# Projections in even half steps, later loads, gelu inputs in score banks, a new order at the end, and exponentials tile by tile

## The chip, the core and the metric

The kernel runs on one core of one Trainium2 chip. Its engines work side by side, each through a queue of its own in program order, and wait for one another by semaphores: TensorE (PE in the profile; its weight loads are PEld), VectorE (DVE), ScalarE (ACT), GpSimd (POOL) and SyncE (SP), which here only issues transfers. The metric is the device time of one launch in microseconds (us).

## What is computed

Two layers, each a gated cross attention of 16 heads and a gated feed-forward, on 4 batches of 512 tokens of width 256. The first feed-forward is a mixture of 8 experts of which each token takes two; the second rounds activations to 8 bits and weights to three values. Cut to what matters:

```python
x = x + tanh(g_xattn[0]) * xattn(layernorm(x), ctx, ctx, Wq, bq, Wk, bk, Wv, bv, Wo, bo)   # layer 0
x = x + tanh(g_ffn[0]) * moe(layernorm(x), router_w, router_b, expert_weights)
x = x + tanh(g_xattn[1]) * xattn(layernorm(x), ctx, ctx, ...)                             # layer 1
x = x + tanh(g_ffn[1]) * ffn(layernorm(x), w1, w2)

def xattn(query, key, value, ...):
    q, k, v = heads(query @ Wq.T + bq), heads(key @ Wk.T + bk), heads(value @ Wv.T + bv)  # 16 heads of 16
    weights = softmax(einsum('bhqd,bhkd->bhqk', q, k) / sqrt(16))
    return einsum('bhqk,bhkd->bhqd', weights, v) @ Wo.T + bo

def ffn(x, w1, w2):
    h = gelu(quant_act(x) @ quant_weight(w1).T)
    return quant_act(h) @ quant_weight(w2).T
```

## The kernel before

The attention of one batch in one layer is a pass: p = 0 to 3 are the batches in layer 0, p = 4 to 7 in layer 1. All passes form one stream of steps G, 16 to a pass; step G treats four heads of a group and one tile of 128 keys. A step has two half steps, an even one and an odd one, with two heads each. `table()` writes the stream out: in each half step come the first score products S of the step that is LEAD = 6 steps ahead (two matmuls of queries by keys into the three banks of psS, whose row maxima VectorE takes), then the second score products T (two matmuls of keys by queries, with rows that subtract the maxima, into the two banks of psT), then, in odd half steps only, the four products PV of the exponentials with the values of the step before. ScalarE takes the exponential of psT once for each half step. The maxima of a group pass GpSimd (M), a transpose on TensorE (MT), ScalarE, and a transfer by SyncE into rows of qs, for which the group's first T waits.

Everything else is put between these by `work_table()`: `put(p, s, item)` places an item behind half step s (0 to 31) of pass p. Its names: SPLIT is a projection of queries (Q) or keys (K) of a pass, in two halves of 128 columns; TensorE makes it in a bank of psX, ScalarE reads it twice (qf, parts), GpSimd forms the low part, SyncE writes both to memory, and RELOAD fetches them stacked for S and T. VV is the projection of values. XT, OT, XB, HT, NT are transposes, OP the output projection, LNC and LNN the layer norm, ST its statistics. ME are the experts' products and MH the splitting of their weights. LD is a load of weights or of a batch (x2, x3), CTX one of context. ABS, WS and QUANT round the weights w1 and w2. F1, HQ, HS, HT and F2 are the second feed-forward, tile by tile of 128 tokens: product into 1024 columns and gelu, maximum and scale, rounding, transposes, product. All pieces but S, T and PV share the two banks of psX in turn. F1 takes psT for tiles 0 and 2 and both banks of psX for tiles 1 and 3.

Work of pass p's batch lies under pass p + 1, so the last batch's feed-forward stands alone behind the stream, in an order written by hand. Ahead of the stream stand the projections of pass 0 and one of pass 1. `due` leaves out a wait that an earlier one on the engine covers.

## Time and profile before

| what | us |
|---|---|
| median of three runs | 811.45 (808.52 to 812.57) |
| the profiled execution, its own time | 810.76 |
| its span, first to last instruction | 809.0 |
| TensorE matmuls busy | 709.5 |
| VectorE busy | 529.0 |
| ScalarE busy | 448.7 |
| GpSimd busy | 168.1 |

The profile is one execution. Busy time of TensorE counts the whole length of pipelined matmuls, so a busy TensorE need not be at its peak. An idle time has what ended it behind an arrow.

### The profile page before, as it was taken

How to read it: one execution, taken by the hardware profiler on the slowest of the kernel's cores; microseconds unless marked ns; L12 is line 12 of the kernel's file. 1: busy time of each engine (PE TensorE's matmuls, PEld its weight loads, DVE VectorE, ACT ScalarE, POOL GpSimd, SP SyncE). 2: the span in 40 equal slices, each digit the busy share in tenths (PEclk: the TensorE clock that was granted, in tenths of full speed). 3: DMA queues.
4: the chain of work that ended last, by engine and by line, in shares of the span. 5: the costliest groups of instructions: out<-in, count | busy, mean ns of one | idle time of the engine just before them, and what ended most of it. 6: DMA issues, size and time to landing. Idle time of an engine off the chain costs nothing.

```text
span 809.0 us, 10145 instructions
## 1 busy us (share of the span) xinstructions
PE 709.5 (88%) x3554; PEld 333.6 (41%) x3554; DVE 529.0 (65%) x1138; ACT 448.7 (55%) x572; POOL 168.1 (21%) x302
## 2 busy tenths in 40 slices
PE   5789898899999999998999999888899888988735
PEld 2423333345554445454544455334344334423413
DVE  3485765567787687868886787573777468755252
ACT  3225555774336633664346633666675677568644
POOL 6333222441001310122011210121301211021041
PEclk9758989999999999999999999898799889979975
DMA  6983618524210501224111510314221403000000
GB/s 227 268 254 131 201 50 253 144 78 113 46 41 28 157 4 38 65 82 79 40 41 40 145 41 17 89 79 118 46 61 41 118 9 87 13 2 15 13 1 26
DMA packets 39922, 66.74 MB, mean 82 GB/s; under 512 B 6080, under 2 KB 14784, under 8 KB 39616
## 3 DMA queue, kind: packets, MB, share of 16 engines
q1 hardware_dynamic: 39024, 65.57, 28.7%
q8 instruction: 28, 0.46, 0.2%
q10 hardware_dynamic: 848, 0.53, 0.2%
q14 instruction: 22, 0.18, 0.1%
HBM read 38.29 MB, written 27.26 MB: 81 GB/s over the span
## 4 chain that ended last, share of the span: by engine, by line
PE 64%; ACT 12%; DVE 11%; issue 6%; POOL 5%; DMA 1%; SPq 0%; POOLq 0%; DVEq 0%; ACTq 0%
PE psO L775 14%; PE psS L747 7%; PE psT L761 7%; PE psX L702 7%; PE psX L836 5%; ACT pt L986 5%; DVE mx L1166 4%; PE psX L812 4%; PE psX L837 4%; PE psX L838 3%; PE psX L722 3%; PE psX L892 2%; DVE xs L1297 2%; PE psX L733 2%; ACT parts L934 1%
## 5 line engine op out<-in xcount | busy, mean ns | idle before, releaser
L1166 DVE TENSOR_REDUCE mx<-psS 128x1 f32<-128x512 f32 x512 | 324.7, 681 | 121.6 <-PE psS L747 121.3
L986 ACT ACTIVATE pt<-psT 128x1024 f32<-128x1024 f32 x256 | 261.6, 1022 | 225.1 <-PE psT L761 222.8
L747 PE MATMUL psS<-ks,qs 48*128 48x512 f32 x512 | 155.4, 519 | 16.6 <-DVE mx L1166 16.0
L775 PE MATMUL psO<-pt,vg 128*32 128x512 f32 x1024 | 148.6, 655 | 0.1
L761 PE MATMUL psT<-qs,ks 50*128 50x512 f32 x512 | 120.6, 444 | 24.1 <-ACT pt L986 22.2
L747 PEld LDWEIGHTS psS<-ks,qs 48*128 48x128 f32 x512 | 61.1, 194 | 128.2 <-issue 70.6
L1297 DVE SCALAR_TENSOR_TENSOR xs<-psX,coef,xs 128x256 f32<-128x256 f32 x128 | 61.8, 483 | 32.3 <-PE psX L838 29.2
L569 POOL TENSOR_TENSOR parts<-qf,parts 128x512 fp32r<-128x512 f32 x32 | 40.8, 1274 | 190.8 <-ACT parts L934 190.8
L761 PEld LDWEIGHTS psT<-qs,ks 50*128 50x128 f32 x512 | 53.3, 196 | 46.8 <-ACT pt L986 44.2
L836 PE MATMUL psX<-moeh,xh 128*128 128x512 f32 x128 | 57.5, 449 | 4.4 <-DVE xs L1297 4.4
L837 PE MATMUL psX<-moel,xh 128*128 128x512 f32 x128 | 51.0, 398 | 0.0
L838 PE MATMUL psX<-moeh,xl 128*128 128x512 f32 x128 | 50.3, 393 | 0.0
L702 PE MATMUL psX<-ctxb,wk 128*128 128x512 f32 x64 | 39.6, 754 | 7.6 <-DMA wk<-in_Wk 7.6
L836 PEld LDWEIGHTS psX<-moeh,xh 128*128 128x128 f32 x128 | 24.1, 189 | 43.6 <-DVE xs L1297 22.5
L643 POOL CAST mp<-mx 128x16 fp32r<-128x16 f32 x32 | 6.7, 208 | 169.6 <-DVE mx L1166 169.3
L943 ACT ACTIVATE xn<-xs,lnw 128x256 f32<-128x256 f32 x60 | 31.8, 590 | 15.8 <-POOL lnw L605 15.7
L658 POOL TENSOR_SCALAR hh<-hh,am 128x1024 f32<-128x1024 f32 x16 | 17.9, 1120 | 107.1 <-DVE am L1338 107.1
L775 PEld LDWEIGHTS psO<-pt,vg 128*32 128x32 f32 x1024 | 20.6, 110 | 43.3 <-issue 42.2
L702 PE MATMUL psX<-xnt,wq 128*128 128x512 f32 x64 | 35.0, 676 | 2.0 <-ACT xnt L956 1.6
L722 PE MATMUL psX<-wv,ctxb 128*128 128x256 f32 x128 | 32.8, 402 | 0.0
L812 PE MATMUL psX<-wo,ont 128*128 128x256 f32 x128 | 31.6, 391 | 0.8 <-ACT ont L979 0.8
L1095 DVE BATCH_NORM_STATS2 st<-xs 128x6 f32<-128x256 f32 x64 | 26.4, 413 | 7.3 <-DMA xs<-in_x 6.6
(128 smaller groups left out, 745.9 us busy)
## 6 DMA issues: line engine op xcount, KB each, us to landing
ks<-kd SPq DMA_DIRECT2D x64, 192.0 KB, 3.7
qs<-qd SPq DMA_DIRECT2D x64, 192.0 KB, 4.6
kd<-parts SPq DMA_DIRECT2D x16, 512.0 KB, 2.8
qd<-parts SPq DMA_DIRECT2D x16, 512.0 KB, 2.7
kd<-parts SPq DMA_DIRECT2D x16, 256.0 KB, 3.0
qd<-parts SPq DMA_DIRECT2D x16, 256.0 KB, 3.5
ctxb<-in_ctxT SPq DMA_DIRECT2D x7, 512.0 KB, 3.4
xs<-in_x SPq DMA_DIRECT2D x4, 512.0 KB, 6.8
```

Source lines behind the costliest of these rows:

```text
L702: i = mm(o, w[:, k, c * P:(c + 1) * P], src[:, k, :], start=k == 0, stop=k == NC - 1)
L722: i = mm(o[:, t * D:(t + 1) * D], ctxb[:, p % 2, k, (2 * half + t) * P:(2 * half + t + 1) * P], wv[l][:, k, :], start=k == 0, stop=k == NC ...
L747: mm(psS[:, i % 3, :], qs[at:at + KR, 2 * g + a, k * P:(k + 1) * P], ks[at:at + KR, 2 * g + a, :], start=True, stop=True).then_inc(pe_s, 1)
L761: i = mm(psT[:, r, :], ks[at:at + KR + MP, 2 * g + half, k * P:(k + 1) * P], qs[at:at + KR + MP, 2 * g + half, :], start=True, stop=True)
L775: i = mm(psO[32 * j:32 * j + 32, :], vg[:, p % 2, k, g * GH + j, :], pt[:, s % RING, j, :], start=k == 0, stop=k == NT - 1, tile_position= ...
L812: i = mm(o[:, t * D:(t + 1) * D], ont[:, k, tt * P:(tt + 1) * P], wo[l][:, k, :], start=k == 0, stop=k == NC - 1)
L836: mm(o, xh[:, k, tok], moeh[:, k, at], start=k == 0, stop=False)
L837: mm(o, xh[:, k, tok], moel[:, k, at], start=False, stop=False)
L838: i = mm(o, xl[:, k, tok], moeh[:, k, at], start=False, stop=k == NC - 1)
L986: a(pt[:, G % RING, 2 * half:2 * half + 2, :], psT[:], ACT.Exp, scale=SCALE).then_inc(a_exp, 1)
L1166: v.tensor_reduce(mx[:, w // GH % 2, r, col:col + 1], psS[:, i % 3, :], AX.X, ALU.max).then_inc(v_max, 1)
L1297: v.scalar_tensor_tensor(out=xs[:, b, t, :], in0=o[:, k * D:(k + 1) * D], scalar=coef[:, t, e:e + 1], in1=xs[:, b, t, :], op0=ALU.mult, op ...
```

## The change

Projections: one query projection ahead of the stream and one under the first S products are taken into the stream; almost all SPLITs of the first two passes, and the key projections of passes 6 and 7, stand behind even half steps. The keys of batches 2 and 3 (for passes 2 and 3) come in pass 0 and at the start of pass 1. VV(1, ·) stands at half steps 8 and 14 of pass 0. Loads: x3, k1, w1, w2, moe0, moe1, o, rt, v1 and q1 are issued later, and ABS, WS and QUANT with them. F1 of tiles 1 and 3 goes into the first two banks of psS; it waits until VectorE has read all S so far, and the next S waits for all gelus so far. The V projections stand behind F1(1) and F1(2). The end has a new order. The exponential of a half step is two ACTIVATEs of 512 columns; each T product signals for itself, and each waits only for the exponential that read its own bank.

```diff
@@ work_table
-    put(lead, 23, ("BOB", ()))
+    put(lead, 24, ("BOB", ()))
-    put(lead, 26, ("LD", ("w1",)))
-    put(lead, 28, ("LD", ("w2",)))
-    put(lead, 29, ("SPLIT", ("Q", 1, 1)))
     for t in range(NT):
         st(0, t, 2, t)
-        st(0, 9 + t, 3, t)
-    put(0, 0, ("LD", ("o",)), ("BIAS", (1, 0)))
-    put(0, 1, ("LD", ("rt",)))
-    put(0, 3, ("LNC", (2, 0, NT)), ("SPLIT", ("K", 1, 0)), ("ABS", (0,)))
-    put(0, 4, ("LD", ("moe0",)))
-    put(0, 5, ("LNN", (2, 0, 2)), ("SPLIT", ("K", 1, 1)), ("ABS", (1,)))
...
-    pair(0, 19, "SPLIT", "Q", 3, step=2)
-    pair(0, 23, "SPLIT", "K", 4, step=2)
...
-    pair(0, 27, "SPLIT", "K", 5, step=2)
...
-    pair(1, 1, "SPLIT", "K", 2, step=3)
-    pair(1, 6, "SPLIT", "K", 3, step=10)
+        st(0, 5 + t, 3, t)
+    put(0, 0, ("SPLIT", ("Q", 1, 0)), ("LD", ("x3",)), ("BIAS", (1, 0)))
+    put(0, 1, ("LD", ("w1",)))
+    put(0, 2, ("SPLIT", ("K", 1, 0)))
+    put(0, 3, ("LNC", (2, 0, NT)), ("LD", ("w2",)))
+    put(0, 4, ("SPLIT", ("Q", 1, 1)), ("LD", ("k1",)))
+    put(0, 5, ("LNN", (2, 0, 2)))
+    put(0, 6, ("SPLIT", ("K", 1, 1)), ("LNN", (2, 2, 4)))
+    pair(0, 7, "XT", step=2)
+    put(0, 8, ("VV", (1, 0)), ("BIAS", (2, 0)), ("LD", ("moe0",)))
+    put(0, 9, ("ABS", (0,)), ("LNC", (3, 0, NT)))
+    pair(0, 10, "SPLIT", "Q", 2, step=2)
+    put(0, 11, ("ABS", (1,)), ("LNN", (3, 0, 2)))
+    put(0, 12, ("LNN", (3, 2, 4)), ("LD", ("moe1",)))
+    pair(0, 13, "XT", step=2)
+    put(0, 13, ("WS", ()))
+    put(0, 14, ("VV", (1, 1)), ("BIAS", (3, 0)))
+    pair(0, 16, "SPLIT", "Q", 3, step=2)
+    put(0, 18, ("LD", ("o",)))
+    pair(0, 20, "SPLIT", "K", 4, step=2)
+    put(0, 23, ("CTX", (2,)))
+    pair(0, 24, "SPLIT", "K", 5, step=2)
+    put(0, 25, ("LD", ("rt",)))
+    put(0, 27, ("CTX", (3,)))
+    pair(0, 28, "SPLIT", "K", 2, step=2)
+    put(0, 29, ("LD", ("v1",)))
+    for q in range(8):
+        put(0, 14 + 2 * q, ("QUANT", (q // 4, q % 4)))
+    pair(1, 0, "SPLIT", "K", 3, step=2)
+    put(1, 4, ("LD", ("q1",)))
...
             if p + 1 >= B + 2:
-                put(p, 1, ("SPLIT", ("K", p + 1, 0)))
-                put(p, 13, ("SPLIT", ("K", p + 1, 1)))
+                put(p, 2, ("SPLIT", ("K", p + 1, 0)))
+                put(p, 12, ("SPLIT", ("K", p + 1, 1)))
...
             for t in range(NT):
-                if p < NP - 1 and t < 2:
-                    put(p, 16, ("VV", (p + 1, t)))
                 put(p, 16, ("F1", (t,)))
+                if p < NP - 1 and t in (1, 2):
+                    put(p, 16, ("VV", (p + 1, t - 1)))
@@ table
-    out += [("LD", (one,)) for one in ("bo", "x2", "k1", "x3")]
+    out += [("LD", (one,)) for one in ("bo", "x2")]
...
-    out += [("SPLIT", ("Q", 1, 0))]
@@ TensorE: S, T, PV
+                    if due(a_f1, n("F1")):
+                        pe.wait_ge(a_f1, n("F1"))
                     mm(psS[:, i % 3, :], qs[at:at + KR, 2 * g + a, k * P:(k + 1) * P], ks[at:at + KR, 2 * g + a, :],
...
-                if due(a_exp, n("T")):
-                    pe.wait_ge(a_exp, n("T"))
...
                 for r in range(2):
                     at = HALF * r
-                    i = mm(psT[:, r, :], ks[at:at + KR + MP, 2 * g + half, k * P:(k + 1) * P],
-                           qs[at:at + KR + MP, 2 * g + half, :], start=True, stop=True)
-                i.then_inc(pe_t, 1)
+                    if due(a_exp, n("T", 2, r) - 1):
+                        pe.wait_ge(a_exp, n("T", 2, r) - 1)
+                    mm(psT[:, r, :], ks[at:at + KR + MP, 2 * g + half, k * P:(k + 1) * P],
+                       qs[at:at + KR + MP, 2 * g + half, :], start=True, stop=True).then_inc(pe_t, 1)
@@ TensorE: F1
-                    for b in range(2):
-                        if due(*last[b]):
-                            pe.wait_ge(*last[b])
-                        last[b] = (a_f1, i + 1)
-                    o = psX
+                    if due(v_max, n("S", 2)):
+                        pe.wait_ge(v_max, n("S", 2))
+                    o = psS
@@ ScalarE: exps
-                if due(pe_t, n("T") + 1):
-                    act.wait_ge(pe_t, n("T") + 1)
...
-                a(pt[:, G % RING, 2 * half:2 * half + 2, :], psT[:], ACT.Exp, scale=SCALE).then_inc(a_exp, 1)
+                for r in range(2):
+                    if due(pe_t, n("T", 2, r) + 1):
+                        act.wait_ge(pe_t, n("T", 2, r) + 1)
+                    a(pt[:, G % RING, 2 * half + r, :], psT[:, r, :], ACT.Exp, scale=SCALE).then_inc(a_exp, 1)
```

The order on TensorE at the beginning, from the transposes of batch 1 on. Before, L702 is a projection, L747 S, L784 MT, L761 T; after, L707, L754, L790 and L768. First the kernel before:

```order
L733 MATMUL psX<-identf,xn 128x128 x8
L702 MATMUL psX<-xnt,wq 128x512 x2
L747 MATMUL psS<-ks,qs 128x512 x18
L784 MATMUL psX<-identf,mp 32x128
L747 MATMUL psS<-ks,qs 128x512 x2
L702 MATMUL psX<-xnt,wq 128x512 x2
L747 MATMUL psS<-ks,qs 128x512 x6
L761 MATMUL psT<-qs,ks 128x512 x2
```

And the changed one:

```order
L738 MATMUL psX<-identf,xn 128x128 x8
L754 MATMUL psS<-ks,qs 128x512 x18
L790 MATMUL psX<-identf,mp 32x128
L754 MATMUL psS<-ks,qs 128x512 x8
L768 MATMUL psT<-qs,ks 128x512 x2
L707 MATMUL psX<-xnt,wq 128x512 x2
L754 MATMUL psS<-ks,qs 128x512 x2
```

Both query projections of pass 1 left the part ahead of the first T; one now stands right behind it.

The order on TensorE around F1 in pass 5 (L874 before, L878 after), with the V projections (L722, L727). Before:

```order
L761 MATMUL psT<-qs,ks 128x512 x2
L722 MATMUL psX<-wv,ctxb 128x256 x4
L874 MATMUL psT<-w1q,xit 128x512 x4
L722 MATMUL psX<-wv,ctxb 128x256 x4
L874 MATMUL psX<-w1q,xit 128x512 x4
L874 MATMUL psT<-w1q,xit 128x512 x4
L874 MATMUL psX<-w1q,xit 128x512 x4
```

After:

```order
L768 MATMUL psT<-qs,ks 128x512 x2
L878 MATMUL psT<-w1q,xit 128x512 x4
L878 MATMUL psS<-w1q,xit 128x512 x4
L727 MATMUL psX<-wv,ctxb 128x256 x4
L878 MATMUL psT<-w1q,xit 128x512 x4
L727 MATMUL psX<-wv,ctxb 128x256 x4
L878 MATMUL psS<-w1q,xit 128x512 x4
```

The V projections moved behind the second and the third F1, and the odd F1 changed banks.

The order on TensorE at the end: transposes of the input (L851, L857), F1, transposes of h (L884, L888) and F2 (L892, L896). Before:

```order
L851 MATMUL psX<-identb,xi 128x128 x4
L874 MATMUL psT<-w1q,xit 128x512 x4
L874 MATMUL psX<-w1q,xit 128x512 x4
L851 MATMUL psX<-identb,xi 128x128 x4
L874 MATMUL psT<-w1q,xit 128x512 x4
L884 MATMUL psX<-identb,hq 128x128 x8
L874 MATMUL psX<-w1q,xit 128x512 x4
L892 MATMUL psX<-w2q,hqt 128x256 x8
```

After:

```order
L857 MATMUL psX<-identb,xi 128x128 x4
L878 MATMUL psT<-w1q,xit 128x512 x4
L857 MATMUL psX<-identb,xi 128x128 x4
L878 MATMUL psS<-w1q,xit 128x512 x4
L878 MATMUL psT<-w1q,xit 128x512 x4
L878 MATMUL psS<-w1q,xit 128x512 x4
L888 MATMUL psX<-identb,hq 128x128 x16
L896 MATMUL psX<-w2q,hqt 128x256 x8
```

All four F1 now stand ahead of the first transposes of h.

## Rows read from the trace of the kernel before

**Rows 1.** The page: engine shares, then clock and transfer rate in 40 slices of the span.
```profile
PE 709.5 (88%) x3554; PEld 333.6 (41%) x3554; DVE 529.0 (65%) x1138; ACT 448.7 (55%) x572; POOL 168.1 (21%) x302
...
PEclk9758989999999999999999999898799889979975
...
GB/s 227 268 254 131 201 50 253 144 78 113 46 41 28 157 4 38 65 82 79 40 41 40 145 41 17 89 79 118 46 61 41 118 9 87 13 2 15 13 1 26
```

**Rows 2.** Stretches: bounds, length, busy us of each engine, clock, DMA share, GB/s.
```profile
53.00:145.00 92.00, 80.10 (x341) 31.09 (x341) 60.52 (x112) 52.67 (x71) 26.48 (x37) 0.89 0.50 161
145.00:239.00 94.00, 89.36 (x447) 44.46 (x445) 66.18 (x151) 49.74 (x67) 21.61 (x30) 0.96 0.30 84
...
328.00:417.00 89.00, 85.23 (x456) 43.48 (x452) 68.26 (x156) 46.06 (x61) 13.89 (x29) 1.00 0.25 61
...
760.00:809.00 49.00, 24.90 (x128) 14.30 (x124) 16.01 (x46) 20.70 (x26) 10.53 (x24) 0.71 0.04 14
```

**Rows 3.** Groups: the exponential; then what T products waited for, us and times.
```profile
L986 ACT ACTIVATE pt<-psT 128x1024 f32<-128x1024 f32 x256 | 261.6, 1022 | 225.1 <-PE psT L761 222.8
...
  ACT pt L986: 66.4, 89
  DMA qs<-mt: 1.5, 2
```

**Rows 4.** The page's issues; then the timeline (start, length) from 25 to 53 us.
```profile
qs<-qd SPq DMA_DIRECT2D x64, 192.0 KB, 4.6
...
25.09 0.78 SPq L516 DMA_DIRECT2D qs<-qd  x2
...
32.80 0.93 PE L747 MATMUL psS<-ks,qs 48*128 48x512 f32 x3
...
45.07 2.84 SPq L526 DMA_DIRECT2D qs<-mt  x4
...
45.40 3.78 PE L702 MATMUL psX<-xnt,wq 128*128 128x512 f32 x4
...
52.97 0.50 PE L761 MATMUL psT<-qs,ks 50*128 50x512 f32 x2 [0.59 <-DMA qs<-mt]
```

**Rows 5.** Timeline of one step with a projection in its odd half.
```profile
120.10 0.50 PE L761 MATMUL psT<-qs,ks 50*128 50x512 f32 x2 [0.56 <-ACT pt L986]
...
120.64 1.02 ACT L986 ACTIVATE pt<-psT 128x1024 f32<-128x1024 f32 x1 [0.60 <-PE psT L761]
...
121.52 1.98 PE L702 MATMUL psX<-ctxb,wk 128*128 128x512 f32 x4
...
123.55 0.69 ACT L933 ACTIVATE qf<-psX,bkc 128x512 f32<-128x512 f32 x1 [1.88 <-PE psX L702]
...
124.70 1.02 ACT L986 ACTIVATE pt<-psT 128x1024 f32<-128x1024 f32 x1
...
125.78 0.49 PE L761 MATMUL psT<-qs,ks 50*128 50x512 f32 x2 [0.57 <-ACT pt L986]
```

**Rows 6.** Timeline beside expert products: an S pair, a T pair, the next product.
```profile
304.48 0.50 PE L747 MATMUL psS<-ks,qs 48*128 48x512 f32 x2
...
304.82 0.40 PE L761 MATMUL psT<-qs,ks 50*128 50x512 f32 x2
...
305.15 0.50 PE L836 MATMUL psX<-moeh,xh 128*128 128x512 f32 x1
```

**Rows 7.** Timeline: two copies of 512 columns on ScalarE, one behind the other.
```profile
764.22 1.08 ACT L979 ACTIVATE ont<-psX 128x512 f32<-128x512 f32 x2 [0.76 <-PE psX L800]
```

**Rows 8.** Timeline: the second F1 product in pass 5.
```profile
561.12 1.02 PE L874 MATMUL psX<-w1q,xit 128*128 128x512 bf16 x4 [0.88 <-DVE vg L1120]
```

**Rows 9.** Timeline at the end: F1(0), F1(3) and the last F2.
```profile
777.82 1.89 PE L874 MATMUL psT<-w1q,xit 128*128 128x512 bf16 x4 [0.69 <-ACT xit L1026]
...
790.42 1.89 PE L874 MATMUL psX<-w1q,xit 128*128 128x512 bf16 x4 [1.12 <-ACT hqt L1062]
...
805.31 1.03 PE L892 MATMUL psX<-w2q,hqt 128*128 128x256 bf16 x8 [1.21 <-ACT hqt L1062]
```

More of the change, by code:

```diff
@@ L191, in work_table @@
     put(NP, 4, ("OP", (1, b, 1)), ("ST", (b, 2)), ("ST", (b, 3)), ("LNC", (b, 2, 4)))
-    put(NP, 5, ("XQ", (0, 2)), ("LNN", (b, 2, 4)), ("XI", (0, 2)), ("XB", (0, 2)), ("XQ", (2, 4)), ("F1", (0,)))
-    put(NP, 5, ("F1", (1,)), ("XI", (2, 4)), ("XB", (2, 4)), ("HQ", (0,)), ("F1", (2,)), ("HS", (0,)), ("HQ", (1,)))
-    put(NP, 6, ("HT", (0,)), ("F1", (3,)), ("HS", (1,)), ("HQ", (2,)), ("F2", (b, 0)), ("XOUT", (b, 0)), ("HT", (1,)))
-    put(NP, 7, ("HS", (2,)), ("HQ", (3,)), ("F2", (b, 1)), ("XOUT", (b, 1)), ("HT", (2,)), ("HS", (3,)))
-    put(NP, 8, ("F2", (b, 2)), ("XOUT", (b, 2)), ("HT", (3,)), ("F2", (b, 3)), ("XOUT", (b, 3)))
+    put(NP, 5, ("XQ", (0, 2)), ("LNN", (b, 2, 4)), ("XI", (0, 2)), ("XB", (0, 2)), ("XQ", (2, 4)), ("XI", (2, 4)))
+    put(NP, 5, ("F1", (0,)), ("XB", (2, 4)), ("F1", (1,)), ("F1", (2,)), ("F1", (3,)))
+    put(NP, 6, *[("HQ", (t,)) for t in range(NT)])
+    put(NP, 6, ("HS", (0,)))
+    for t in range(NT):
+        if t + 1 < NT:
+            put(NP, 6, ("HS", (t + 1,)))
+        put(NP, 6, ("HT", (t,)))
+        if t:
+            put(NP, 6, ("F2", (b, t - 1)), ("XOUT", (b, t - 1)))
+    put(NP, 6, ("F2", (b, NT - 1)), ("XOUT", (b, NT - 1)))
     return at
@@ L1036, in f1 @@
                     act.wait_ge(v_quant, 16)
-                a(hh[:, t, :], (psX if t % 2 else psT)[:].rearrange("p a b -> p (a b)"), ACT.Gelu,
+                a(hh[:, t, :], (psS if t % 2 else psT)[:, 0:2, :].rearrange("p a b -> p (a b)"), ACT.Gelu,
                   scale=am[:, 2, t:t + 1]).then_inc(a_f1, 1)
```

32 lines of the change are left out of this document (8 added, 24 removed).

## The prediction

> **What bounds the kernel now.** I read the page's engine shares first: TensorE is busy for 88% of the span, VectorE for 65%, ScalarE for 55%, and the clock line shows TensorE at half its clock (1.2 GHz) in part of the slices at the beginning, again and again from 500 us on, and at the end [rows 1]. Then the stretches, one by one [rows 2]. The reader is to see that passes are not alike: the pass of group of layer 0 between 328 and 417 us keeps TensorE busy for 85 of 89 us at full clock, while the first pass (53 to 145) has 12 us without a matmul and a mean clock of 0.89, and the last 49 us have half of their time empty. So work that TensorE does in the middle is paid in full, and what can be saved is idle or slow time at the two ends, in the first pass, and in layer 1. Third, the groups: one exponential of 1024 columns takes 1.02 us, and TensorE stood idle 66 us in 89 places because a second score product waited for the exponential before it [rows 3].
>
> **Ahead of the first exponential.** The first S product comes at 32.80 us, behind a query projection of batch 1; a second one (3.78 at half clock) sits between S products at 45.40; the first T product is issued at 52.97, when the transfers of the maxima, issued from 45.07 on, have landed [rows 4]. The change takes both projections out. The first S product then waits for its operands alone: their load is issued at 25.09, and its median landing is 4.6 us, so about 30.1 [rows 4]; this saves 2.7 us. The other projection saves 3.7. The maxima then leave some 3 us sooner, into queues that no longer hold the 1 MB load of w1 (nor wk1, x3), which is what made them take 5 us after issue; I take 2 us. BOB, put one half step later, still finds its operand there. The first T product comes at about 47: **−6.0 us**. Ends: −2.7 if the maxima land as late as now, −7.
>
> **Projections in even half steps.** A step of the stream is two half steps; only the odd one has the four PV products. A step with a projection in the odd half step reads [rows 5]: T at 120.10, projection at 121.52, ScalarE's two reads of it from 123.55, the exponential only at 124.70, the next odd T at 125.78. That is 5.68 us, and in the even half TensorE has nothing but S and T while two ScalarE instructions and the exponential pass one after the other. With the projection in the even half, worked from the same rows: T at 0, projection 0.33 to 2.25 (as long as from 121.52 to the 123.44 that 123.55 follows), S and T of the odd half to 2.9 (0.34 for a pair [rows 6]), ScalarE's two reads from 2.36 to 3.51, PV to 3.95, S, and T at 4.3 to 4.67, when the second of the two exponentials of 3.51 has ended. The period is 4.67 us: **1.0 us less** for each. A step without a projection takes 1.62 in its even half (T to exponential 0.54, exponential 1.02, back to T 0.06, as from 120.10 to 120.64 and from 124.70 to 125.78 [rows 5]) and 1.66 in its odd one (T, PV, S), so 3.28.
>
> First pass: ten projections and two V projections are moved to even half steps (−10.1, −1.8), and four more are added there, two that stood ahead of the stream and two keys of batch 2 (4 × 1.39 = +5.6). The transposes of the outputs (NT) stand in even half steps, were hidden under the exponential's wait and are no longer in three steps (+2, by their size). The late loads come now: x3, w1, w2, wk1 and three projections' writes, some 5 MB, within 15 us, at the 254 to 268 GB/s that the page shows as the most, in its second and third slice [rows 1]; the maxima of the second group queue behind them, and I take +2 (ends 0 and +10). The stretch from 53 to 64 us, where TensorE waited for exponentials at half clock, is filled with matmuls and should come back to full clock sooner, −3. Sum **−5** (ends +4, −10).
>
> Second pass (145 to 239): it takes 94 us, the third of its kind 89 [rows 2]. What it has more are two projections net and the experts' splitting, and the two projections are what leaves: **−4** (ends −1, −6). The moved loads of q1, v1, rt and o come 10 or more half steps before their use and cost nothing; their issues on SyncE (0.5 to 0.9 us each) stand behind no transfer of maxima that is due.
>
> Layer 1: four key projections go from odd to even half steps, at the 1.0 us above, a little less where the quantisation stands beside them: **−3.5** (ends 0, −4).
>
> **Gelu inputs in score banks.** Now the second F1 product waits until VectorE has emptied the bank of the V projection (0.88 us idle at 561.12) [rows 8]. After, it writes psS and needs no such wait, but the first F1 product has lost the V projection that covered the exponential, the first S product waits for all four gelus, and the table load behind them still gates the next exponential. Two passes have V projections: **−1** (ends +3, −2).
>
> **The end.** Now the product F1(0) is issued at 777.82, F1(3) only at 790.42, held back behind ScalarE's work on tile 0, and the last F2 at 805.31 [rows 9]. After, the four follow one another at a little under their 1.89 us (half clock) with one wait for the second half of the transposed input, so F1(3) at about 785 and its gelu done at 788. Then ScalarE has four subtractions and four copies of 1024 columns, each about as long as an exponential of that size (1.02 [rows 3]), one behind the other; the last copy ends at 797.7 and the last F2 starts at 798. Against 805.31 that is **−6** after losing a little at its start (ends −3, −8).
>
> **Tile by tile.** This touches 256 exponentials. Two of 512 columns follow each other at 0.50 (the pair of copies took 1.08 together [rows 7]) and last 1.10 against 1.02. TensorE's queue is in order: what follows the second T product still waits for the second half exponential, so a single wait gets 0.08 longer, 89 × 0.08 = +7 at most [rows 3]. Gain comes only where one wait follows another, since the next first half can start 0.4 sooner; I count 12 such places along the exponentials, −5. In layer 1 ScalarE is the busier engine, and 0.08 more for each half step there is some +3, half of it on the path. Where the wait is already met, it costs nothing: an S pair has a wait and an increment on each product and takes 0.34, as a T pair has one and takes 0.33 [rows 6]. Sum **+2.5** (ends −10, +10). What stands against this part is the Trainium skill, "TensorE: Matmul & The Clock Gate", section "The cost: per-tile semaphore tail": one increment on the last of several packed matmuls is enough, and each further one costs about 26 ns. By it the 256 new increments would cost at most 6.7 us, an estimate from that page, and the time would be about 795; the S and T pairs here show no such difference in their issue, so the sum leaves it out.
>
> **Sum.** 6 + 5 + 4 + 3.5 + 1 + 6 − 2.5 = 23 us. The profiled execution took 810.76 us (span 809.0), the median of three runs is 811.45; both stand within 0.1%. Prediction: 811.45 − 23 = **788.5 us**.
>
> **Rivals.** (1) TensorE is the bound and even half steps are no better than odd ones: only the two ends and the F1 term count, −12 in all, +2.5: **802 us**. For it: 88% busy. Against it: the 5.68 us step has 4.25 us of matmul work (1.92, the PV's 0.99, two S at 0.34, two T at 0.33). Chance 0.15. (2) The late loads clog the queues in the first pass: maxima and score operands land 8 to 12 us late in sum, **798 us**. For it: 268 GB/s is the most in any slice [rows 1], and by their sizes some 10 MB would now move between 50 and 90 us, which is that rate all the time. Against: in the kernel before, whose loads are crowded too, T waited for maxima 1.5 us in two places [rows 3]. Chance 0.15. (3) The halves help at every wait: 0.42 less in each of 89 places, −37 in place of +2.5, and **750 us**. Against: the queue is in order. Chance 0.05. (4) Slower: the wait between the two T products parts them, so that they no longer run side by side in the array. Then the second costs 0.33 us more [rows 6] at up to 256 places, +84 us, **872 us**; it decides from 0.09 us per pair on. Against: the S pairs have the same wait and stay together. Chance 0.06. (5) The first forecast: 0.55, its own range 780 to 796. The remaining 0.04 are small failures of several parts, near no change.
>
> **Chances.** A measurement of this kernel can tell about 0.5% from no change, 4 us. Faster by more: all but the fourth rival and the rest, 0.89. Within: 0.05. Slower by more: 0.06. The range holds the forecast and the first two rivals with the bounds of the unknown terms: 774 to 804.
>
> **What would show it.** The first T product at 47 us and not 53; exponential starts 4.7 us apart per step in the first pass; that pass ending near 134 us; the second 90 us long; key projections in layer 1 without a T wait behind them; the last F2 some 13 us after F1(3), and 20 us after F1(0) instead of 27.5. T pairs in the experts' stretches must still start together. I would be wrong if the clock line showed longer half-clock stretches than before in the first pass, or if ScalarE's work in layer 1 became one unbroken row.

## The result, and the profile after

The changed kernel took **771.57 us** (median of four, 770.73 to 773.67) against 809.99 us of the kernel before (median of four, 806.96 to 812.57): ratio 0.953, 95% interval 0.949 to 0.957. It gained 38 us where 23 were forecast, and lies 2.4 us below the range. Measured once more, with both kernels on one chip, it took 772.82 us against 806.81 (ratio 0.959, 0.954 to 0.963), 34 us less. The profiled execution took 771.77 us, its span is 770.0.

The page after, as [rows 1], and the exponential and what T products waited for, as [rows 3] (line, shapes, count, busy us, mean ns, idle time before; behind it what T products waited for, us and times):

```profile
PE 687.2 (89%) x3550; PEld 333.8 (43%) x3554; DVE 530.8 (69%) x1138; ACT 458.9 (60%) x828; POOL 166.8 (22%) x302
...
PEclk9769999998999999999999999999999999989977
...
L991 ACT ACTIVATE pt<-psT 128x512 f32<-128x512 f32 x512 | 277.3, 596 | 202.7 <-PE psT L768 201.4
```

```profile
  ACT pt L991: 21.7, 58
  issue: 0.4, 2
  DMA qs<-mt: 0.2, 1
```

The second row to compare is the clock line. Of the five 8s and 7s that the kernel before has between 500 and 700 us one 8 is left, from 674 us on. VectorE, ScalarE and GpSimd do the same work as before, ScalarE with its exponentials in twice as many instructions and 10 us more busy time; TensorE's busy time fell by 22 us with the same matmuls (four records are missing), because fewer of them ran at half clock. The stretches of the changed kernel, as [rows 2] (bounds, length, busy us of PE, PEld, DVE, ACT, POOL, clock, DMA share, GB/s): passes 0, 1, 3, 5, 6, 7 and the end.

```profile
46.00:131.00 85.00, 81.05 (x355) 32.33 (x354) 63.07 (x112) 58.46 (x111) 30.24 (x41) 0.96 0.71 229
131.00:224.00 93.00, 88.61 (x440) 44.58 (x440) 66.09 (x150) 49.28 (x96) 20.10 (x29) 0.94 0.27 71
313.00:402.00 89.00, 85.31 (x456) 43.92 (x452) 68.29 (x156) 47.52 (x93) 13.91 (x29) 1.00 0.25 61
491.00:576.00 85.00, 76.44 (x436) 35.94 (x435) 59.49 (x120) 63.18 (x108) 20.06 (x37) 0.98 0.28 84
576.00:655.00 79.00, 69.81 (x414) 33.09 (x412) 57.37 (x114) 58.51 (x99) 12.89 (x26) 1.00 0.26 69
655.00:728.00 73.00, 61.55 (x350) 27.00 (x350) 40.76 (x87) 54.74 (x91) 10.00 (x22) 0.95 0.06 17
728.00:770.00 42.00, 24.09 (x133) 13.77 (x132) 16.30 (x47) 21.19 (x27) 10.53 (x24) 0.79 0.05 16
```

Passes 5 and 6 of the kernel before, which the prediction hadn't looked at as stretches:

```profile
506.00:601.00 95.00, 84.42 (x437) 36.88 (x435) 60.10 (x119) 62.64 (x77) 20.07 (x37) 0.87 0.27 75
601.00:685.00 84.00, 73.97 (x411) 32.66 (x412) 56.78 (x113) 56.78 (x66) 12.95 (x26) 0.92 0.24 63
```

From the starts of the first exponential of each pass:

| | forecast | before | after | difference |
|---|---|---|---|---|
| first exponential at | −6 | 53.5 | 46.8 | −6.8 |
| pass 0 | −5 | 91.5 | 84.9 | −6.6 |
| pass 1 | −4 | 94.1 | 93.0 | −1.1 |
| passes 2 to 4 | 0 | 267.1 | 266.7 | −0.4 |
| passes 5 and 6 | −4.5 | 179.3 | 163.6 | **−15.7** |
| pass 7 | 0 | 73.7 | 73.3 | −0.4 |
| last exponential to the end | −6 | 49.9 | 41.8 | −8.1 |

**How far one execution speaks.** Beside the experiments below the kernel before ran 85 times; spans from 792.3 to 814.7 us, with the same instructions. Half-clock time, which is 2 × (1 − mean clock) × span, went from 89 to 145 us in them, and the span follows it on a line: 756.8 + **0.40** × half-clock time, correlation 0.96. So 1 us more at half clock goes with 0.40 us more of the span, and a difference of a few us in one pass of one execution may be the clock alone.

The line is read from executions of one program and doesn't say which of the two causes the other; the runs with fillers below do that in part. Taken over to other kernels it is an estimate: in the changed kernel's ten executions, whose half-clock time differs by 11 us only, it can't be seen (correlation 0.38).

Each kernel is compared with the kernel before on the same chip; where a part is taken out, the 771.57 us of the changed kernel, with which it is compared too, were measured apart, and a difference of 1 us there says nothing. The changed kernel has 65 to 67 us of half clock on average, the one before 115 to 124. The printed ratios leave out executions over 1.5% above the fastest of a kernel, which cuts off the longer ones of the kernel before where they spread as here; medians of all executions stand beside them.

### The profile page after: what moved, and what is told of

Its sections match the earlier page's. It is cut to its first block, busy times and chain, and to the rows that moved or that the text cites. A ratio compares the mean times of both kernels' runs of the same rounds, so it can differ in the third digit from the quotient of the medians.

```text
span 770.0 us, 10396 instructions
## 1 busy us (share of the span) xinstructions
PE 687.2 (89%) x3550; PEld 333.8 (43%) x3554; DVE 530.8 (69%) x1138; ACT 458.9 (60%) x828; POOL 166.8 (22%) x302
## 4 chain that ended last, share of the span: by engine, by line
PE 60%; DVE 14%; ACT 10%; issue 8%; POOL 6%; DMA 2%; SPq 0%; POOLq 0%; ACTq 0%; DVEq 0%
PE psO L781 11%; PE psS L754 8%; PE psX L707 7%; DVE mx L1171 6%; PE psT L768 6%; PE psX L842 5%; PE psX L818 4%; PE psX L843 4%; PE psX L844 4%; PE psX L727 3%; POOL parts L574 2%; DVE xs L1302 2%; ACT pt L991 2%; PE psX L738 1%; ACT qf L937 1%
## 5 line engine op out<-in xcount | busy, mean ns | idle before, releaser
L991 ACT ACTIVATE pt<-psT 128x512 f32<-128x512 f32 x512 | 277.3, 596 | 202.7 <-PE psT L768 201.4
L1171 DVE TENSOR_REDUCE mx<-psS 128x1 f32<-128x512 f32 x512 | 325.0, 681 | 88.2 <-PE psS L754 88.0
L754 PE MATMUL psS<-ks,qs 48*128 48x512 f32 x512 | 152.9, 512 | 19.1 <-DVE mx L1171 13.3
L781 PE MATMUL psO<-pt,vg 128*32 128x512 f32 x1024 | 139.7, 618 | 0.2 <-ACT pt L991 0.2
L768 PE MATMUL psT<-qs,ks 50*128 50x512 f32 x512 | 136.9, 423 | 2.8 <-ACT pt L991 2.7
L754 PEld LDWEIGHTS psS<-ks,qs 48*128 48x128 f32 x512 | 60.7, 190 | 137.6 <-issue 71.9
L768 PEld LDWEIGHTS psT<-qs,ks 50*128 50x128 f32 x512 | 64.7, 188 | 22.7 <-ACT pt L991 19.0
L707 PE MATMUL psX<-ctxb,wk 128*128 128x512 f32 x64 | 35.8, 691 | 7.8 <-DMA wk<-in_Wk 7.8
L818 PE MATMUL psX<-wo,ont 128*128 128x256 f32 x128 | 33.3, 407 | 0.8 <-ACT ont L983 0.8
L707 PE MATMUL psX<-xnt,wq 128*128 128x512 f32 x64 | 32.2, 629 | 1.2 <-ACT xnt L960 0.8
L727 PE MATMUL psX<-wv,ctxb 128*128 128x256 f32 x128 | 32.5, 400 | 0.0
L1125 DVE TENSOR_TENSOR vg<-psX,bvb 128x512 f32<-128x512 f32 x16 | 11.0, 690 | 31.0 <-PE psX L727 31.0
```

The costliest lines, as they stand in the source:

```text
L707: i = mm(o, w[:, k, c * P:(c + 1) * P], src[:, k, :], start=k == 0, stop=k == NC - 1)
L754: mm(psS[:, i % 3, :], qs[at:at + KR, 2 * g + a, k * P:(k + 1) * P], ks[at:at + KR, 2 * g + a, :], start=True, stop=True).then_inc(pe_s, 1)
L768: mm(psT[:, r, :], ks[at:at + KR + MP, 2 * g + half, k * P:(k + 1) * P], qs[at:at + KR + MP, 2 * g + half, :], start=True, stop=True).then ...
L781: i = mm(psO[32 * j:32 * j + 32, :], vg[:, p % 2, k, g * GH + j, :], pt[:, s % RING, j, :], start=k == 0, stop=k == NT - 1, tile_position= ...
L818: i = mm(o[:, t * D:(t + 1) * D], ont[:, k, tt * P:(tt + 1) * P], wo[l][:, k, :], start=k == 0, stop=k == NC - 1)
L991: a(pt[:, G % RING, 2 * half + r, :], psT[:, r, :], ACT.Exp, scale=SCALE).then_inc(a_exp, 1)
```

## Experiments: each part alone, and each part taken out

Four parts alone on the kernel before, then three taken out of the changed kernel, and the end alone. The edits are pieces of the diff above; here their first lines.

**Tile by tile alone.**

```diff
-                a(pt[:, G % RING, 2 * half:2 * half + 2, :], psT[:], ACT.Exp, scale=SCALE).then_inc(a_exp, 1)
+                for r in range(2):
...
+                    a(pt[:, G % RING, 2 * half + r, :], psT[:, r, :], ACT.Exp, scale=SCALE).then_inc(a_exp, 1)
```

> The kernel before, with exponentials and T products tile by tile and nothing else. Open is where the 15.7 us come from that the first two passes of layer 1 with a feed-forward beside them (5 and 6) gained, against 4.5 forecast (keys 3.5, F1 banks 1). Theory K, the key projections in even half steps bring them: this part is worth nothing or the small loss of the sum, 810 to 813 us, and passes 5 and 6 keep their 94.6 and 84.7 us. Rival T, tile by tile brings them, because ScalarE starts 0.4 us sooner after each T wait and TensorE stays busy enough for its full clock: passes 5 and 6 together at least 8 us shorter, 798 to 803 us. Rival F (banks of F1) says of this run what K says. If the wait parts the T products, over 830 us.

Measured: 812.31 us against 810.02 (ratio 1.007, 1.002 to 1.012): a loss of 2.3, as the term of the sum said. In its profile passes 5 and 6 took 90.6 and 83.3 us, 5.4 less in sum than in the profile of the kernel before, where theory T asked for 8. Theory T falls.

**Key projections alone.**

```diff
-                put(p, 1, ("SPLIT", ("K", p + 1, 0)))
-                put(p, 13, ("SPLIT", ("K", p + 1, 1)))
+                put(p, 2, ("SPLIT", ("K", p + 1, 0)))
+                put(p, 12, ("SPLIT", ("K", p + 1, 1)))
```

> The kernel before, with the key projections of passes 6 and 7 behind half steps 2 and 12 in place of 1 and 13, and nothing else. Theory K: most of the gain of passes 5 and 6, 9 to 12 us, 798 to 801 us, with the half-clock stretches at 518, 545, 569, 631 and 654 us mostly gone. By the forecast's own term, 3.5 us, 806.5 us, with the half-clock stretches as before: then the rest of the gain needs another part. Rivals T and F: 806 to 808 us.

Measured: 801.53 us against 810.02 (0.990, 0.982 to 0.998): 8.5 us. Passes 5 and 6 took 84.8 and 78.8 us, what they take in the changed kernel, with 10 us of half clock in place of 38. Over the whole kernel its four executions have 120 us of half clock on average against 124, so by the slope of 0.40 the clock is under 2 us of the 8.5: what went in these two passes stood elsewhere (in passes 0, 4, 7 and at the end of its profile).

**F1 in score banks alone**, with its order of V projections.

```diff
-                    o = psX
+                    o = psS
```

> The kernel before, with F1 of tiles 1 and 3 in the banks of the first score products, and V projections behind the second and third F1, and nothing else. Forecast's term: 1 us, 809 us. Rival F, these banks bring the excess: passes 5 and 6 together 7 to 10 us shorter, 800 to 803 us. Theories K and T: 808 to 811 us.

Measured: 800.78 us against 810.02 (0.989, 0.983 to 0.994): 9.2 us, where 1 was forecast. Its half-clock time is 102 us against 124, worth 8.8 us at 0.40; at equal half-clock time nothing is gained. In its profile passes 5 and 6 took 172.7 us, no less than in the three profiles with neither this part nor the keys that follow the kernel before (172.1 to 173.9). Shorter are the end, 45.8 us against 49.9, where F1 writes score banks too, and passes 0 and 1, which the part doesn't touch; the profiled execution is the shortest of its ten.

**First two passes and the start alone.**

```diff
-    out += [("SPLIT", ("Q", 1, 0))]
...
+    pair(0, 10, "SPLIT", "Q", 2, step=2)
```

> The kernel before, with the new placing of projections and loads in the first two passes and ahead of them, and nothing else. In the changed kernel the first exponential came 6.8 us sooner, pass 0 was 6.6 and pass 1 was 1.1 us shorter. If these belong to this part: 14.5 us, 795.5 us, and passes 2 to 7 as before. If pass 1 gained its forecast 4 us here and tile by tile took 3 back: 792.5 us. Theory C, one part's gain depends on the others through the clock: the time differs from 795.5 us by over 3 us in passes that this part doesn't touch.

Measured: 790.13 us against 810.02 (0.979, 0.969 to 0.988): 19.9 us. First exponential at 46.76, pass 0 86.1 us, pass 1 91.7. Pass 5, not touched by this edit, took 88.0 us instead of 94.6: the clock again (half-clock time 101 us against 124).

**The changed kernel without tile by tile.**

```diff
-                for r in range(2):
...
+                a(pt[:, G % RING, 2 * half:2 * half + 2, :], psT[:], ACT.Exp, scale=SCALE).then_inc(a_exp, 1)
```

> The changed kernel, with one exponential of 1024 columns and one signal of a T pair for each half step as before. Forecast's term for tile by tile was a loss of 2.5 us: 769 us without it. Theories K and F: 768 to 773 us, passes 5 and 6 keep their gain. Rival T: passes 5 and 6 lose at least 8 us of it, 780 to 784 us.

Measured: 770.51 us (before on that chip: 806.69). That is 1.1 us below the changed kernel, within the spread of either (768.11 to 773.72 and 770.73 to 773.67). Passes 5 and 6 keep their gain (84.5 and 78.1).

**The end alone.**

```diff
+    put(NP, 5, ("F1", (0,)), ("XB", (2, 4)), ("F1", (1,)), ("F1", (2,)), ("F1", (3,)))
```

> The kernel before, with the new order behind the last pass and nothing else, so F1 of tiles 1 and 3 keeps the two psX banks. From the last exponential to the end the changed kernel took 41.8 us against 49.9. If the order alone brings that: 8 us, 802 us. If it needs the score banks for F1 (tile 1 would then wait in psX for the transposes' readers): 2 to 6 us, 804 to 808 us.

Measured: 800.12 us against 806.69, 6.6 less by the medians, but a printed ratio of 1.000 (0.994 to 1.007): the times alone don't show the gain. The profile does: from the last exponential to the end 41.3 us, against 49.9 in the kernel before and 48.0 to 50.7 in seven other kernels with the old order and the old banks of F1. The score banks aren't needed for it.

**The changed kernel with its keys in odd half steps.**

```diff
-                put(p, 2, ("SPLIT", ("K", p + 1, 0)))
-                put(p, 12, ("SPLIT", ("K", p + 1, 1)))
+                put(p, 1, ("SPLIT", ("K", p + 1, 0)))
+                put(p, 13, ("SPLIT", ("K", p + 1, 1)))
```

> The changed kernel, with the key projections of passes 6 and 7 back behind half steps 1 and 13. Forecast's term: 3.5 us, 775 us. Theory K: 9 to 12 us lost, 781 to 783 us, and the half-clock stretches of passes 5 and 6 come back. Rivals T and F: 774 to 776 us.

Measured: 782.56 us, 11.0 above the changed kernel. Passes 5 and 6 took 92.8 and 84.4 us, with half clock from 503 to 513, 530 to 537, 609 to 619 and 639 to 642.

**The changed kernel with F1 in its old banks.**

```diff
-                    o = psS
+                    o = psX
```

> The changed kernel, with F1 of tiles 1 and 3 back in both banks of psX, and the V projections ahead of their F1. Forecast's term 1 us and some of the end: 773 to 775 us. Rival F: passes 5 and 6 lose 7 us or more, and 779 to 783 us. Theories K and T: under 776 us.

Measured: 772.84 us, 1.3 above the changed kernel and within the spread of either. So the F1 part is worth 9 us alone and about 1, if anything, on top of the others. One reason is in the profiles: 4 of the 9 us stand in the end, and the new order there brings its 8.6 us without the banks. That the rest is half clock which the keys remove as well (the stretches at 569 and 654 us before are gone in its profile) is argued and not shown, since passes 5 and 6 as a whole are no shorter in it.

## Experiments: direct wait or clock

The trace shows what stands ahead of the fall at 518 us. The kernel before, TensorE in pass 5: the maxima's transpose (L784) waits for GpSimd, which is late because the key projection of half step 1 (L702) went through it, and an OT (L800) waits for a copy.

```profile
509.29 1.98 PE L702 MATMUL psX<-ctxb,wk 128*128 128x512 f32 x4
...
517.31 0.28 PE L784 MATMUL psX<-identf,mp 128*32 128x128 f32 x1 [1.02 <-POOL mp L646]
518.48 1.12 PE L800 MATMUL psX<-identf,on 128*128 128x128 f32 x4 [0.88 <-ACT ont L979]
519.52 0.80 PE L747 MATMUL psS<-ks,qs 48*128 48x512 f32 x2
520.11 0.63 PE L761 MATMUL psT<-qs,ks 50*128 50x512 f32 x2
520.67 1.93 PE L775 MATMUL psO<-pt,vg 128*32 128x512 f32 x8
```

The same place with the keys alone moved:

```profile
522.54 0.27 PE L784 MATMUL psX<-identf,mp 128*32 128x128 f32 x1 [0.33 <-POOL mp L646]
523.03 0.66 PE L800 MATMUL psX<-identf,on 128*128 128x128 f32 x4 [0.22 <-ACT ont L979]
523.62 0.51 PE L747 MATMUL psS<-ks,qs 48*128 48x512 f32 x2
...
524.37 1.06 PE L775 MATMUL psO<-pt,vg 128*32 128x512 f32 x8
```

The waits are 1.3 us shorter, and that is the direct gain at this place. But eight PV matmuls take 1.06 instead of 1.93: behind the longer idle the clock fell to its lower level (1.2 GHz), and everything until 525 ran at half speed. It doesn't fall each time. Eight profiles have this pair of waits (0.96 to 1.05 us, then 0.88). In four of them the clock fell there, for 7 or 10 us (the kernel before, the changed one with keys in odd half steps, and the second key and the V order alone, below); in the other four (tile by tile, F1, the start and the end, each alone) it didn't. In none of the twelve profiles without the pair did it fall there. To part wait and clock, I put products that nothing reads ahead of the instructions that wait.

**Fillers in pass 5, keys in odd half steps.**

```diff
+            def fill(o, k):
+                for _ in range(k):
+                    mm(o[:, 0:P], identf[:], identf[:], start=True, stop=True)
...
                 o = bank("MT")
+                fill(o, {21: 7, 22: 8}.get(i, 0))
...
                 o = bank("OT")
+                fill(o, {9: 6}.get(n("OT"), 0))
```

> The changed kernel with its key projections of passes 6 and 7 back in odd half steps (782.56 us measured, 11 above the changed one), and 21 additional products of a 128x128 identity (0.13 us each) that nothing reads, in three places of pass 5 where TensorE stood idle and after which the clock fell: 7 ahead of the MT at 502 us (0.96 us idle), 6 ahead of the second OT (0.88), 8 ahead of the MT at 529 (1.19). They write a bank of psX that the real one overwrites. Clock theory: what the odd half steps cost is mostly the slower clock behind such idle places. Then the half-clock stretches 503 to 513 and 530 to 537 vanish, those of pass 6, where nothing is added, stay, and the time is 775 to 778 us. Direct theory: the key projections cost through waits alone, and the additional 2.8 us of work hides or costs: 782 to 785 us.

Measured: 783.64 us: no gain, the time that the direct theory gave. One filler took 0.23 us, not 0.13 (the trace has two records for each, of 0.12), so they overran the idle time. Still pass 5 had no half clock (row below) and took 87.4 us instead of 92.8, with 4.8 us of fillers in it; pass 6, without fillers, kept its half clock and took 86.4.

```profile
491.00:579.00 88.00, 81.16 (x480) 40.17 (x477) 59.94 (x120) 64.09 (x109) 20.15 (x37) 1.00 0.29 82
579.00:665.00 86.00, 76.37 (x411) 34.79 (x412) 56.67 (x114) 58.56 (x98) 13.00 (x26) 0.92 0.24 62
```

**The same fillers in the kernel before.** The same edit on the kernel before.

> The kernel before with the same 21 additional products at the same three instructions, in front of which it stood idle for 1.02, 0.88 and 1.26 us. Clock theory: the half-clock stretches at 518 (7 us) and 545 (3 us) go, 3 to 5 us less than before by half of their length. Direct theory: no gain, up to 2 us more.

Measured: 802.01 us against 805.93 (0.995, 0.991 to 1.000); half-clock time 104 against 117. In the direction of the clock theory, but the interval still holds no change. Pass 5 took 87.4 us in its profile.

**Fillers of the right length.**

```diff
+                fill(o, {21: 4, 22: 5}.get(i, 0))
...
+                fill(o, {9: 4}.get(n("OT"), 0))
...
+                    if i in (411, 423, 429, 431):
+                        b = n.piece() % 2
...
+                        fill(psX[:, b, :], 2 if i > 423 else 1)
```

> The changed kernel with its key projections in odd half steps again, and additional products of the identity once more, now at their measured length of 0.23 us each: 4, 4 and 5 in pass 5 where 7, 6 and 8 overran the idle time, and 6 in all ahead of four S products of pass 6 (411, 423, 429 and 431) that waited 0.32 to 0.54 us. Without fillers pass 5 took 92.8 and pass 6 84.4 us, with the first fillers 87.4 and 86.4 (with half-clock stretches of 7 and 7 us in pass 6), with the keys in even half steps 84.9 and 78.7. Clock theory: no half clock in pass 5, 86 us; 3 us or none in pass 6, 80 to 82 us; 774 to 778 us in all. Direct theory: 782 to 785 us.

Measured: **778.03 us**, 4.5 below the kernel without fillers (782.56, on another chip; 775.83 to 781.89 against 780.62 to 786.01), with additional work in it. The fillers of the OT stand behind the wait for its bank, so the 0.88 us ahead of it stayed idle, and still the clock didn't fall there. Passes 5 and 6, first without fillers, then with them:

```profile
491.00:584.00 93.00, 83.46 (x435) 37.40 (x433) 59.52 (x120) 63.96 (x109) 20.06 (x37) 0.91 0.27 76
584.00:668.00 84.00, 76.85 (x412) 34.71 (x412) 56.72 (x114) 58.17 (x98) 12.95 (x26) 0.92 0.24 62
```

```profile
492.00:580.00 88.00, 80.86 (x464) 38.45 (x457) 59.15 (x118) 64.32 (x110) 20.08 (x37) 0.98 0.29 84
580.00:661.00 81.00, 72.62 (x423) 34.34 (x424) 57.16 (x113) 58.49 (x98) 12.95 (x26) 1.00 0.26 67
```

In these two profiles work that nobody needs made the passes 8.2 us shorter: 92.8 + 84.4 without, 87.9 + 81.1 with. The other 5.4 us to the changed kernel's 84.9 + 78.7 are what the fillers can't give back: the direct waits, and whatever of the fillers isn't hidden. So of the 13.6 us of the keys in these profiles about 60% is the clock. This pair exaggerates: the profiled execution without fillers is the longest of its four (786.01 us), the one with them the shortest (775.83). Of the medians' 11.0 us the fillers gave 4.5 back, about 40%.

**The two halves of the keys.** Only `put(p, 1, …)` to `put(p, 2, …)`, and only `put(p, 13, …)` to `put(p, 12, …)`, on the kernel before.

> The kernel before with only the first key projection of passes 6 and 7 moved, from half step 1 to 2. Both together measured 8.5 us. If the late maxima are what costs (the projection of half step 1 goes through ScalarE and GpSimd just ahead of the maxima, and MT at 517 us waits 1.02 us for GpSimd): most of it is here, 802 to 804 us, and MT no longer waits there. If both halves count alike through longer steps: 4 us, 805 to 807 us.

> The kernel before with only the second key projection moved, from half step 13 to 12. If the late maxima of the first are what costs: 807 to 810 us. If both count alike: 805 to 807 us.

Measured: 802.50 and 801.97 us against 805.13 (0.996, 0.992 to 1.000; 0.997, 0.992 to 1.002): 2.6 and 3.2 us. Neither outweighs the other. The profiles part them at the place above: with the first half moved both waits are gone, with the second alone they stand (1.05 and 0.88 us). Since the second, from which nothing or little was expected, brings as much, these waits are not the main cost of the keys. Together the halves measured 8.5; their sum is 5.8, and with a few us of spread in each it can't be said whether they are more than additive.

**V order without the banks.**

```diff
-                if p < NP - 1 and t < 2:
-                    put(p, 16, ("VV", (p + 1, t)))
                 put(p, 16, ("F1", (t,)))
+                if p < NP - 1 and t in (1, 2):
+                    put(p, 16, ("VV", (p + 1, t - 1)))
```

> The kernel before with the V projections of passes 6 and 7 behind the second and third F1 in place of ahead of the first two, F1 in its old banks. With the new banks too this measured 9.2 us below before, against 1 forecast. If the order brings that: 801 to 804 us. If the banks do: 808 to 812 us.

Measured: 812.68 us against 805.93, 6.8 more by the medians, with a ratio that holds no change (1.005, 0.999 to 1.011). The V projection now needs a bank of psX that the second F1's gelu still reads:

```profile
558.69 1.99 PE L722 MATMUL psX<-wv,ctxb 128*128 128x256 f32 x8 [1.53 <-ACT hh L1037]
...
564.15 1.02 PE L874 MATMUL psX<-w1q,xit 128*128 128x512 bf16 x4 [0.88 <-DVE vg L1120]
...
568.71 0.50 PE L761 MATMUL psT<-qs,ks 50*128 50x512 f32 x2 [1.44 <-ACT pt L986]
```

With the banks (the part alone) both of the first waits are gone, the first S waits 1.21 us for the gelus, and T waits 0.17:

```profile
554.71 0.50 PE L749 MATMUL psS<-ks,qs 48*128 48x512 f32 x2 [1.21 <-ACT hh L1037]
...
557.05 0.51 PE L763 MATMUL psT<-qs,ks 50*128 50x512 f32 x2 [0.17 <-ACT pt L986]
```

The banks make the order possible; the order alone gains nothing, and by the medians it loses.

## Experiments: the two ends, and a faster version

**Fillers at both ends of the changed kernel**, at twice the right length, then at the right one.

```diff
+                fill(o, {12: 46}.get(n("XB tiles"), 0))
...
+                fill(o[:, 0, :], {12: 7, 13: 8}.get(i, 0))
```

> The changed kernel with such additional products ahead of the stream (16 ahead of the transposes at 26.4 us, 14 ahead of the first S) and behind it (4, 5 and 5 ahead of the last NT, OT and OP, 46 ahead of the XB at 747 us, 7 and 8 ahead of F1 of tiles 0 and 1, 14 ahead of the first HT), each number the idle time there by 0.13 us. Clock theory: the half-clock stretch 29 to 49 us and most of the 20 us of them behind 735 go, and with them 8 to 14 us: 758 to 764 us. Rival: so few columns do not hold the clock, or the places wait for other engines anyway: 769 to 773 us.

> The changed kernel with additional products at its two ends again, at their measured 0.23 us: 10 and 7 ahead of the first S, 3, 3 and 3 ahead of the last NT, OT and OP, 27 ahead of XB, 4 and 5 ahead of F1 of tiles 0 and 1, 8 ahead of HT. With twice the length the ends ran at full clock but 2 us late at the start and 4 us late at XB, and the time was 776.8 us. Clock theory: without that delay 766 to 769 us, the lowest of all kernels here. Rival, the ends are bound by other engines: 770 to 773 us.

Measured: 776.83 us (before on its chip 805.93), 5 more than the changed kernel, where 6 to 14 less were expected, and 769.95 us (before 805.13), between the ranges of the two theories (766 to 769, 770 to 773). With the right length the tail took 38.3 us instead of 41.8 (40.4 to 43.0 in the other profiles with the new end and no fillers there). At the start the fillers brought nothing: half clock still stood from 34 to 51 us, and the first exponential came at 48.36 instead of 46.75, which isn't theirs, since in the second profile of the changed kernel, without fillers, it came at 48.44. So I kept them behind the stream alone, and left tile by tile out:

```diff
+                fill(x, {31: 3}.get(i, 0))
...
+                fill(o, {14: 3}.get(n("OT"), 0))
...
+                fill(o, {14: 3}.get(n("OP"), 0))
...
+                fill(o, {12: 27}.get(n("XB tiles"), 0))
...
+                fill(o[:, 0, :], {12: 4, 13: 5}.get(i, 0))
...
+                fill(o, {12: 8}.get(i, 0))
```

> The changed kernel without tile by tile (770.51 us measured, 1.1 below the changed one) and with the additional products behind the last exponential alone (3, 3, 3, 27, 4, 5 and 8 as before). At both ends they brought the tail from 41.8 to 38.3 us and the first exponential from 46.75 to 48.36. Clock theory: 3 to 4 us below the changed kernel by the tail and 1 by the exponentials, 766 to 768 us. Rival: the tail's gain is given back as in the median of the run with both ends (769.95): 769 to 771 us.

> The changed kernel once more, on the same chip as the run beside it, so that the two can be compared and the spread of its half-clock time is seen: 768 to 774 us.

Measured on one chip: **765.89 us** (763.80 to 767.35, six runs) for the version with fillers, 772.82 us (771.70 to 775.04, six runs) for the changed kernel: 6.9 us less, and the two don't overlap. About 1 of it may be tile by tile, by the run that took this out. The end, the changed kernel first (F1 of tiles 0 to 3 and the last F2), then this version (fillers, L689, then F1 of tiles 0 and 3 and the last F2):

```profile
748.61 1.49 PE L878 MATMUL psT<-w1q,xit 128*128 128x512 bf16 x3 [1.09 <-ACT xit L1031]
...
751.88 1.86 PE L878 MATMUL psS<-w1q,xit 128*128 128x512 bf16 x4 [1.36 <-ACT xit L1031]
753.54 1.91 PE L878 MATMUL psT<-w1q,xit 128*128 128x512 bf16 x4
755.25 1.21 PE L878 MATMUL psS<-w1q,xit 128*128 128x512 bf16 x4
...
766.28 1.05 PE L896 MATMUL psX<-w2q,hqt 128*128 128x256 bf16 x8 [0.24 <-ACT hqt L1067]
```

```profile
735.21 6.19 PE L689 MATMUL psX<-identf 128*128 128x128 f32 x54
...
743.89 1.03 PE L889 MATMUL psT<-w1q,xit 128*128 128x512 bf16 x4
...
748.99 1.04 PE L889 MATMUL psS<-w1q,xit 128*128 128x512 bf16 x4 [0.34 <-ACT hh L1054]
...
759.88 1.05 PE L909 MATMUL psX<-w2q,hqt 128*128 128x256 bf16 x8 [0.24 <-ACT hqt L1079]
```

An F1 takes 1.03 instead of up to 1.91 us, and the whole end is at full clock (1.00 against 0.79 in the stretch).

## Why the prediction was right or wrong, point by point

- **The sum: wrong, 38 us against 23 (34 on one chip).** Every term had its sign right. What was mis-sized most is layer 1. The prediction had named the half-clock slices from 500 us on in its first paragraph and then priced the key projections at full clock, 1.0 us for each. The kernel before had 37 us of half clock in passes 5 and 6 (the clock of 0.87 and 0.92 in its two stretches says 25 + 13), the changed one 3 (0.98 and 1.00); by the slope of 0.40 that is 13.6 us, and I gave it none. The clock enters the sum only with 3 us in pass 0 and inside the end.

  The profiled execution of the kernel before makes this gain look larger than it is. With tile by tile, the start or the end alone, which leave these passes' projections and F1 as they were, the two took 173.9, 173.8 and 172.1 us, each with 20 us of half clock; with the 179.3 of the kernel before the mean is 174.8. Six profiles with both edits took 162.6 to 163.9, each with 3 us. That is 11.4 us where 4.5 were forecast, 8.5 of them by the slope.

  Over the whole kernel 53 us less of half clock (119 us on average over the 85 executions, 66 in the changed kernel's ten) are some 21 us by the same slope, an estimate, more than half of the gain. What is left of the 34 us is some 13, and the sum had 20 without its clock term: the terms of waits and work were too large as a whole (pass 1 most plainly), and the clock covered that too.
- **Layer‑1 keys: −3.5 forecast, −8.5 alone and −11.0 taken out.** The failed step: the term priced four longer steps and put the clock behind the odd half steps at nothing. The waits behind it were there (MT's wait for GpSimd 1.02 to 0.33 us), and the part that fillers can't give back, at most 5.4 us in the profiles, is near the term. How much is clock depends on the kernel: taken out, the part costs 21 us of half clock (66 to 87), some 8 of the 11.0 us by the slope; alone it removes 4 us on average, under 2 of the 8.5. Why it gains more than its term there too stays open.
- **F1 banks: −1 forecast, −1.3 taken out, −9.2 alone.** Near in the changed kernel, where the difference isn't clear of the spread. Alone it shows how one gain can be taken by either of two parts, here at the end of the kernel. The wait of 0.88 us did go, and the first S pays 1.21 for the gelus, as said; that T waits 0.17 instead of 1.46 behind them I had not seen.
- **Start: −6 forecast, −6.8.** First T at 45.93 where 47 was said, first S at 29.47 against 30.1. The pieces of the term (2.7, 3.7 and 2) add up to 8.4, and why it is 6 isn't said.
- **Pass 0: −5 forecast, −6.6; its end at 131.7 where 134 was said.** Near in sum, and in part by luck. The step was off: from one step to the next exponential starts are 4.6 to 6.5 us apart, 5.3 on average (5.7 before), where 4.67 was said for a step with a projection. And the clock counted for more than its 3 us. In nine profiles without this part pass 0 took 88.2 to 95.7 us, in the eleven with it 84.9 to 86.1. Where the half clock in the pass is alike, 13 us without the part and 12 with it, it took 88.2 and 86.0: 2 us are the steps, and most of the rest is half clock, 20 us in the profile of the kernel before and 6 in the changed one.
- **Pass 1: −4 forecast, −1.1.** Over the profiles the pass took 89.4 to 93.3 us with this part (eleven, mean 91.7) and 91.0 to 95.8 without (nine, mean 93.9): 2.2 us, half of the term. Which wait took the rest no run was aimed at; it stays open.
- **End: −6 forecast, −8.1**, with the new order alone −8.6. The last F2 starts 17.7 us after F1(0), where 20 was said, and 11.0 after F1(3), where 13 was said. The prediction's own row gives less than 13: eight instructions of 1.02 us behind 788 end at 796.2, not at 797.7.
- **Tile by tile: +2.5 forecast, +2.3 alone, +1.1 taken out (not clear of the spread).** What T waited for exponentials fell from 66.4 us to 21.7 in the changed kernel, to 40.3 with this part alone and to 32.5 with all but this part, and still the part costs time: by the term a shorter wait ahead of T comes back as one behind it, since what follows needs the second exponential; the runs fit that and don't show it by itself. The T pairs stay together: beside expert products the next product starts 0.33 us after the pair, as in [rows 6], now with a wait and an increment on each.

```profile
289.54 0.50 PE L754 MATMUL psS<-ks,qs 48*128 48x512 f32 x2
289.87 0.40 PE L768 MATMUL psT<-qs,ks 50*128 50x512 f32 x2
290.20 0.50 PE L842 MATMUL psX<-moeh,xh 128*128 128x512 f32 x1
```

  The part alone costs 2.3 us (interval 0.2% to 1.2%), of which the longer pair of exponentials (1.08 to 1.11 against 1.02 us) explains some. By the page "TensorE: Matmul & The Clock Gate" of the Trainium skill, section "The cost: per-tile semaphore tail", 256 more increments would cost up to 6.7 us, an estimate. The trace shows nothing of them.
- **The rivals.** (1), only the ends count, 802 us: fell; passes 5 and 6 alone gained 11 to 15.7 us. (With the F1 term that it names its sum is 13 and not 12.) (2), late loads clog the queues: fell; T waited 0.2 us for the transfer of maxima in the whole span, at 229 GB/s in pass 0. (3), halves help at every wait, 750 us: fell with the part alone. (4), parted T products: fell.
- **The range.** Its low end came from adding bounds of waits. A row for "half clock in layer 1 goes" was missing: 37 us × 0.5, the ratio at which a busy TensorE slows, would have put it at some 770.

## What to carry to other kernels

Read the clock by stretches, and price each half-clock stretch that the change may remove, not only the wait ahead of it: here 1 us at half clock goes with 0.40 us of the span, and behind two idle places of 1.0 and 0.9 us on TensorE the clock was at half for 7 to 10 us in four of eight profiles. Look at more than one profile before you price it, since the half-clock time of one pass differs between executions. Gains don't add up where parts alone take the same time, of the clock or of the end; take parts out of the changed kernel as well as doing them alone. Where a wait at a known place can't be removed, fill it with products that nothing reads, no longer than the idle time: fillers of about twice that length cost what they saved, or more.

## What the runs showed that I had not expected

- The same program varies by 22 us (792.3 to 814.7 in 85 executions), and its half-clock time goes with that: slope 0.40, correlation 0.96. The changed kernel varies by 4 in ten executions, with little more than half of its half-clock time.
- Pass 7 took 70.5 to 75.9 us over all profiles, with no edit in it but the exponentials; the profile of 70.5 has 3 us of half clock in it (the version with fillers in the tail), one of 75.7 has 20 (fillers at both ends). It follows the half clock in it; what sets that no run was aimed at.
- An additional product of a 128x128 identity in f32 takes 0.23 us in two records of 0.12, and with 27 of them in 6 us of waiting TensorE stayed at full clock.
